# A recurrence with two small VectorE operations rewritten: one tensor from SBUF and a scalar by row in place of two tensors

## The reference

```python
x = x + xattn(layernorm(x), ctx, ctx)      # 8 heads of 64, causal, matrix-memory recurrence
x = x + experts(layernorm(x))              # 16 experts choose 2 tokens of the 32 at each position
```

```python
cs = cumsum(log_f)
log_D = where(tril, cs[s] - cs[t], -inf) + ig[t]
max_log_D = max over t of log_D
D = exp(log_D - max_log_D)
C = (q @ k.T / 8) * D
normalizer = maximum(abs(C.sum(-1)), exp(-max_log_D))
h = (C / (normalizer + 1e-6)) @ v ; then a norm within each head, times out_w
```

## Time and profile before

| what | value |
|---|---|
| median of 3 runs | 1745.97 us (1745.84 to 1746.75) |
| profiled execution, its own time | 1738.19 us |
| its span in the trace | 1736.4 us |
| busy, share of the span: PE, DVE, POOL, ACT | 90%, 81%, 73%, 66% |
| granted TensorE clock, mean | 0.979 |
| recurrence stage | to about 1115 us of the span |

### The profile page before, as it was taken

How to read it: one execution, slowest core, us unless ns; L and a number is a source line. 1 busy time by engine, 2 the same in 40 slices (tenths; PEclk the granted TensorE clock), 3 DMA queues, 4 the chain that set the end, 5 groups by cost and what they waited for, 6 DMA issues and landing times. The chain is left out here.

```text
span 1736.4 us, 58211 instructions
## 1 busy us (share of the span) xinstructions
PE 1554.1 (90%) x21967; PEld 1257.7 (72%) x22095; DVE 1398.5 (81%) x2826; ACT 1154.4 (66%) x2775; POOL 1262.1 (73%) x1235
## 2 busy tenths in 40 slices
PE   4899999999999999999999999679999969998983
PEld 3777777777777777777777777579999945555541
DVE  2588888888888888888888888768766458999998
ACT  3677777777777777777777776422334338888873
POOL 1477787777778777777877877757887527979764
PEclk9899999999999999999999999889999989999998
DMA  6133322233222333222323211173565354777787
GB/s 219 46 99 100 99 94 93 93 103 102 94 93 93 99 100 100 94 93 93 103 97 98 93 51 39 45 294 112 169 205 147 98 121 112 213 231 218 224 228 208
DMA packets 82020, 217.72 MB, mean 125 GB/s; under 512 B 13136, under 2 KB 14544, under 8 KB 72784
## 3 DMA queue, kind: packets, MB, share of 16 engines
q1 hardware_dynamic: 71504, 180.42, 33.4%
q0 software_dynamic: 10240, 33.56, 6.7%
HBM read 146.82 MB, written 67.11 MB: 123 GB/s over the span
## 5 line engine op out<-in xcount | busy, mean ns | idle before, releaser
L315 POOL TENSOR_TENSOR rec_hn<-rec_hn,rec_out_w 128x512 f32<-128x512 f32 x128 | 183.3, 1432 | 124.5 <-DVE rec_hn L747 124.5
L293 POOL TENSOR_TENSOR rec_hrs<-rec_harg,rec_minus_half 128x8 f32<-128x8 f32 x128 | 253.9, 1983 | 10.0
L767 DVE TENSOR_TENSOR rec_x_ring<-rec_x_ring,rec_hn 128x512 f32<-128x512 f32 x128 | 88.7, 693 | 121.8 <-POOL rec_hn L315 121.4
L543 ACT ACTIVATE rec_d<-rec_l_ps 128x512 f32<-128x512 f32 x256 | 151.4, 592 | 52.2 <-PE rec_l_ps L447 50.8
L713 DVE TENSOR_TENSOR rec_c<-rec_s_ps,rec_d 128x512 f32<-128x512 f32 x256 | 166.4, 686 | 13.8 <-ACT rec_d L543 4.9
L1013 PE MATMUL exp_q_ps<-exp_wqkv,exp_rows_t 128*128 128x192 f32 x1024 | 177.1, 327 | 0.0
L1344 POOL TENSOR_TENSOR out_x_half<-out_x_half,ln_b 128x512 f32<-128x512 f32 x104 | 132.7, 1282 | 54.3 <-DVE out_z L1520 53.5
L964 POOL DMA_INDIRECT exp_x_rows<-x_scratch,rowid x128 | 135.0, 1055 | 45.8 <-issue 24.2
L467 PE MATMUL rec_o_ps<-rec_v_one,rec_c 128*64 128x65 f32 x4096 | 151.9, 226 | 16.8 <-DVE rec_c L713 16.8
L1013 PEld LDWEIGHTS exp_q_ps<-exp_wqkv,exp_rows_t 128*128 128x128 f32 x1024 | 165.4, 191 | 0.1
L1073 ACT ACTIVATE exp_rows_t<-exp_t_ps 128x512 f32<-128x512 f32 x128 | 69.4, 594 | 139.5 <-PE exp_t_ps L1001 139.5
(11 more groups left out here) (217 smaller groups left out, 4417.2 us busy)
## 6 DMA issues: line engine op xcount, KB each, us to landing
rec_x_ring<-in_x SPq DMA_DIRECT2D x128, 256.0 KB, 2.9
rec_ctx_ring<-in_ctx SPq DMA_DIRECT2D x128, 256.0 KB, 3.0
x_scratch<-rec_x_ring SPq DMA_DIRECT2D x128, 256.0 KB, 2.0
out_x_half<-x_scratch SPq DMA_DIRECT2D x104, 256.0 KB, 5.0
out<-out_x_half SPq DMA_DIRECT2D x104, 256.0 KB, 5.6
exp_wqkv<-in_wqkv SPq DMA_DIRECT2D x4, 1536.0 KB, 8.9
v_all<-x_scratch SPq DMA_DIRECT2D x24, 256.0 KB, 5.0
out<-v_all SPq DMA_DIRECT2D x24, 256.0 KB, 5.4
```

The source lines that it names most:

```text
L293: nc.gpsimd.tensor_tensor(hrs[:, G % 2], harg[:, G % 2], mhalf[:], ALU.pow).then_inc(hrs_done, 1)
L315: nc.gpsimd.tensor_tensor(h, h, w8[:], ALU.mult).then_inc(hw_done, 1)
L543: nc.scalar.activation(dst[:].rearrange("p k s -> p (k s)"), l_ps[:], ACT.Exp).then_inc(l_read, 1)
```

## The change

`input_offsets` becomes two tensor_scalar instructions, one for each chunk, each on 128x1 elements: the mean as the tensor, the inverse deviation as a scalar by row (one value for each partition), and the constant -1. The diagonals become four tensor_scalar instructions, one for each chunk, each on 8x8 elements: the identity as the tensor, the chunk-end maximum as the scalar by row. Only the last of each group signals. Nothing else moves.

```diff
         def input_offsets(G):
             i = G % 4
             dve.wait_ge(x_pow, G // 2 + 1)
-            vec.scalar_tensor_tensor(xrn[:, i:i + 2, 1], xagg[:, i:i + 2, 0], -1.0, xrn[:, i:i + 2, 0], ALU.mult, ALU.mult
-                                     ).then_inc(x_rs, 1)
+            vec.tensor_scalar(xrn[:, i, 1:2], xagg[:, i, 0:1], xrn[:, i, 0:1], -1.0, ALU.mult, ALU.mult)
+            vec.tensor_scalar(xrn[:, i + 1, 1:2], xagg[:, i + 1, 0:1], xrn[:, i + 1, 0:1], -1.0, ALU.mult, ALU.mult
+                              ).then_inc(x_rs, 1)
...
                 vec.tensor_tensor_scan(mrow[:], sm_ps[0:NH, :], floor[:], LOWEST, ALU.max, ALU.max
                                        ).then_inc(sm_read, 1)
                 small(dve, sm_read, key)
-                vec.tensor_tensor(mend[:], mrow[:, P - 1::P].unsqueeze(2).broadcast_to([NH, NC, NH]),
-                                  ident[0:NH, 0:NH].unsqueeze(1).broadcast_to([NH, NC, NH]), ALU.mult).then_inc(mend_done, 1)
+                for c in range(NC):
+                    end = vec.tensor_scalar(mend[:, c, :], ident[0:NH, 0:NH], mrow[:, (c + 1) * P - 1:(c + 1) * P], None,
+                                            ALU.mult)
+                end.then_inc(mend_done, 1)
```

## The result

The changed kernel takes 1762.39 us in the median (1758.62 to 1766.23, 4 runs) against 1746.36 (1745.84 to 1748.31, 4 runs) of the kernel before: slower, by a ratio of 1.009 with a 95% interval of 1.0065 to 1.0115. The profiled execution took 1758.62 us, its span is 1756.8 us.

What follows compares the result with a forecast made beforehand. PE was taken as the bound, standing still once a sequence for DVE's L713. Offsets 0 plus diagonals 28 x 0.39 = 10.9 us made +11 us on the median of 1745.97, so 1757.0 us, range 1748 to 1765.

Steps and rivals of the forecast that it cites:

- Offsets, 0: DVE's input offsets: the residual behind them waits for POOL's L315 anyway, so 0, ends -0.01 and +0.13 us a sequence.
- The hold: First of four diagonals on DVE is held by POOL's L278 as L795 was, taking about 1.07 us.
- Who comes first: If the first diagonal starts ahead of POOL's L278, the second is held in its place; the sum is the same.
- The further starts: Three more diagonals on DVE after the hold, 0.13 us each: +0.39 us a sequence, ends +0.21 and +0.63.
- The upper end: Further diagonals on DVE do not overlap, 0.21 us each: +0.63 us a sequence, 17.6 us in all.
- One for one to PE: DVE's delay passes fully to PE's L467 waiting for L713: 28 x 0.39 = 10.9 us, wait 15.8 to about 27.
- the sum: Whole kernel: offsets 0 plus diagonals 10.9, so +11 us on the median of 1745.97, giving 1757.0 us.
- the third rival: Diagonals on DVE: held, and each waits for the last one's end; 17.6 us more, 1763.6 us; chance 0.08.
- The second rival: Diagonals on DVE: not held, 0.52 us in place of 1.00; 12.5 us faster, 1733.5 us; chance 0.16.

Runs made afterwards that it cites:

- diagonals only: Kernel before with only the diagonals changed to four tensor_scalar on 8x8: 1757.14 us, ratio 1.0082.
- the pair with nine elements: Kernel before with four nine-element tensor_scalar diagonals, the source as one run of 9 (1764.97 us) or as 3 rows of 3 (1735.73 us).
- nine in one run: Kernel before with the diagonals as four tensor_scalar on nine elements each, source and output one run of 9: 1764.97 us, ratio 1.0098.
- the run with the diagonals on POOL: Kernel before with the diagonals' single tensor_tensor moved from DVE to POOL, behind L278: 1719.36 us, ratio 0.9869.
- rows of three: Kernel before with four nine-element tensor_scalar diagonals, source copied as 3 rows of 3 at a pitch of 4: 1735.73 us, ratio 0.9917.
- eight diagonals: Changed kernel with eight 8x8 diagonals instead of four, the second four into a copy nobody reads: 1779.33 us, ratio to before 1.0195.
- the wide offset: Changed kernel with the first of the two offset instructions on two elements instead of one: 1764.90 us, ratio to before 1.0093.
- twelve memsets ahead: Changed kernel with 12 tiny DVE memsets more at its start: 1757.44 us, ratio to before 1.0073.

## Why the prediction was right

The forecast was 1757.0 us with a range of 1748 to 1765 and slower at 0.78; measured were 1762.39. By the differences, +11 was forecast and +16 came.

- *Offsets, 0.* Right by themselves, shown by the run with them alone (1.0002). Each takes 205 ns, starts lie 0.12 us apart, and the time freed became a wait for L315 (109 waits where I had said about 112, the new ones mostly of 0.72 to 0.74 us). What the forecast did not have: together with the diagonals their 64 instructions move the rest of DVE's program, and seven pauses fall where diagonals only has three.
- *The hold.* Right: the first of four takes 1.05 us and ends with L278 in nearly all sequences. The row on which I had built it, L1223, fits. That the layout of the source decides is now shown by the pair with nine elements, and fits the skill's rule; I had named its even counts only, and the nine in one run are held by its other half, odd and equal. My reading of L1230 as a doubled rate stays unproven: the two rows that I compared also differ in where their source lies, SBUF or PSUM.
- *Who comes first.* The order did not turn: L797 starts at 513.22, still 0.01 us behind L278, and so in nearly all sequences.
- *The further starts, 3 x 0.13 = 0.39 us.* Measured 1.37 - 1.00 = 0.37 us: three starts at 0.13 make 0.40, less 0.03, since the second diagonal starts 0.97 us behind the held one where the moments had started 1.00 behind L795. The upper end, by which each waits for the last one's end, falls with it: durations of 0.21 us at distances of 0.13. The rule of the Trainium skill that I had cited for it (VectorE: DVE Perf Modes, "The DRAIN you can't avoid") does not describe these instructions. The same section adds that a next instruction that is not held starts earlier, which I had left out and which the traces bear out.
- *One for one to PE.* PE's wait rose to 26.6 us in the stretch where I had said about 27. The distance of scans grew by 0.38 us (33.52 to 33.90). Times 28, as I counted, that is 10.6 us; times 31, 11.8. The run with the diagonals on POOL shows the same link in the other direction.
- *What the sum lacked.* Between the scans 14.4 us were lost. 0.38 x 31 = 11.8 are the step above, which I had multiplied by 28 sequences only. 7 x 0.34 = 2.4 us are the pauses, which I had not foreseen at all. The rest of the 16 us lies within the scatter of the later stages and in clock drops, which the recurrence in the profiled execution of the changed kernel does not have but others do. So the time came out nearer to the 1763.6 of the third rival than to the forecast; that this rival is wrong is seen from the distances of starts, not from the time. That these extras stayed within the range is luck: no term of the sum stood for them.
- *The second rival (not held, 12.5 us faster)* is what the rows of three made true: 14.5 us faster. Its arithmetic held (0.46 us a sequence where it had 0.48); its condition was not met by the change.

## What to carry to other kernels

In this kernel a short DVE instruction on two SBUF tensors, or a tensor_scalar whose one SBUF tensor lies in one run (2, 8 and 9 elements were tried), lasted until the POOL instruction that had started before it had ended: up to 1.07 us for one that takes 0.2. A duration far above the smallest of its line, with its end at the end of a POOL instruction, is the sign. Taking away one of two tensors did not help, as 8 elements in a run were held too. Two things did: another layout of the source (rows of 3 against a run of 9, 14.5 us faster than before), and giving the work to POOL, the engine that held it up and that has idle time just then (23 us faster). Several small instructions in place of one cost a start each, 0.13 us, once DVE is what PE waits for. And look first at what stands behind the held instruction: the freed offsets were worth nothing, since the next in line waited for the same POOL instruction.

## What had not been expected

**Behind a longer stall of PE its clock sometimes drops.** In the kernel with eight diagonals some sequences take 35.84 us where 34.3 is the rule. Its table of stretches around one of them (us; busy of PE, PEld, DVE, ACT, POOL; granted clock; DMA share; GB/s):

```profile
211.00:213.00 2.00, 0.98 (x34) 0.80 (x34) 1.93 (x5) 1.68 (x6) 0.00 (x0) 1.00 0.00 0
213.00:214.00 1.00, 0.82 (x23) 0.78 (x24) 1.00 (x6) 0.00 (x0) 0.00 (x0) 1.00 0.00 0
214.00:215.00 1.00, 0.68 (x16) 0.62 (x14) 1.00 (x4) 0.58 (x2) 0.24 (x1) 0.54 0.06 16
215.00:216.00 1.00, 0.99 (x5) 0.52 (x4) 0.89 (x2) 0.60 (x3) 1.00 (x1) 0.50 0.00 0
216.00:217.00 1.00, 1.00 (x17) 0.94 (x16) 0.55 (x1) 0.60 (x1) 0.92 (x3) 0.50 0.00 0
217.00:218.00 1.00, 1.00 (x10) 0.80 (x7) 0.96 (x3) 0.00 (x0) 1.00 (x1) 0.75 0.00 0
218.00:220.00 2.00, 1.79 (x22) 1.36 (x22) 1.16 (x4) 1.97 (x5) 0.64 (x1) 1.00 0.90 289
```

PE's wait in it:

```profile
213.18 1.50 PE L467 MATMUL rec_o_ps<-rec_v_one,rec_c 128*64 128x65 f32 x32 [1.20 <-DVE rec_c L713]
```

PE stood still for 1.2 us, and 0.9 us later the granted clock fell from 1.00 (2.4 GHz) to 0.50 (1.2 GHz) for 3.4 us, which made the sequence 1.5 us longer (1.4 in the other kernels). Such drops, between 140 and 1050 us, are found in the profiled executions with PE's long wait and not in the others: 4 with eight diagonals (waits of 1.2 us), 2 with nine in one run, 1 with diagonals only, 1 with the wide offset, 2 with twelve memsets ahead, 0 and 2 in the two profiles of the changed kernel; 0 before, with the offsets only, with rows of three, and in both kernels with the diagonals on POOL. All twelve start 0.7 to 0.95 us behind the end of a wait for L713 of 1.06 to 1.20 us. But most such waits have no drop behind them, nor has the longest, 1.4 us at 619.8 us with nine in one run. So the number is a matter of the execution, and the longer stall goes with it; that it is the cause of each drop is not shown. It would account for part of the wider scatter of the changed kernel (1758.62 to 1766.23) and for what the eight diagonals cost between the scans: 13.3 us of starts and 4 x 1.5 = 6.0 of drops, less the 2.4 of pauses that this kernel does not have, is 16.9 of the 17.9 measured.

**Pauses that depend on the place in the instruction stream** cost the changed kernel 2.4 us, and went when twelve instructions were put ahead. Those of 0.28 to 0.33 us stand only at every 128th place of DVE's stream, so two kernels that differ by a few small instructions can differ by them alone. What they are the profile does not say, and it was not tried further.
